# A two-layer graph network: a third set of buffers for the gathered rows of the edge network, with gathers issued three groups ahead

## What is computed

```python
h = concat([n_embed[senders], n_embed[receivers]], axis=-1)   # senders = src, receivers = dst
h = tanh(h @ W0 + b0)            # 512 -> 406
h = tanh(h @ W1 + b1)            # 406 -> 323
h = h @ W2 + b2                  # 323 -> 256
h = h * (e_embed @ Wg)           # e_embed: 50000 x 128
return segment_mean(h, senders, 50000)
...
x = layernorm(x + edge_network(x), axis=-1)
```

## Time and profile before

| | us |
|---|---|
| median of three timed executions | 4805.3 |
| lowest, highest of them | 4802.85, 4808.88 |
| profiled execution, first to last instruction (its span; no other time of it is given) | 4813.1 |
| busy: TensorE / VectorE / ScalarE / GpSimd | 3972.5 / 3729.6 / 3089.0 / 2981.9 |
| first gather of the edge network starts | 2698.73 |
| last scatter-add starts | 4504.97 |

### The profile page before, as it was taken

The page is one execution under the profiler, slowest core; times in us unless marked ns, Lnnn a source line. Parts: engine busy times, 40 slices in busy tenths (PEclk is TensorE's granted clock), DMA queues, the critical chain, the costliest instruction groups (busy, mean ns, idle before and its releaser), DMA issues. The chain is left out here.

```text
span 4813.1 us, 84225 instructions
## 1 busy us (share of the span) xinstructions
PE 3972.5 (83%) x23546; PEld 3291.7 (68%) x23546; DVE 3729.6 (77%) x11631; ACT 3089.0 (64%) x7157; POOL 2981.9 (62%) x2765
## 2 busy tenths in 40 slices
PE   5899999977777499999999799999999999999200
PEld 3466666655555399999999687777788778777200
DVE  6899999978888699898989476666666666666564
ACT  6866666645555266666666477776777767776575
POOL 1055556567777355555555377777777778777322
PEclk9999999988999699999999899999999999999655
DMA  4255554558666499999999577766767766766696
GB/s 105 51 171 169 168 171 167 169 148 212 199 201 202 151 360 364 349 365 353 365 359 362 175 152 154 153 149 153 152 150 153 154 152 149 153 150 152 218 394 261
DMA packets 717533, 1002.80 MB, mean 208 GB/s; under 512 B 186862, under 2 KB 591298, under 8 KB 704182
## 3 DMA queue, kind: packets, MB, share of 16 engines
q0 software_dynamic: 160768, 323.45, 30.3%
q10 hardware_dynamic: 245565, 375.01, 21.6%
q1 hardware_dynamic: 310861, 300.30, 19.8%
HBM read 567.01 MB, written 431.82 MB: 208 GB/s over the span
## 5 line engine op out<-in xcount | busy, mean ns | idle before, releaser
L1468 PE MATMUL bank<-w0r,n_x1T 128*128 128x406 f32 x4704 | 903.3, 351 | 41.1 <-ACT n_pa L1516 38.9
L1468 PEld LDWEIGHTS bank<-w0r,n_x1T 128*128 128x128 f32 x4704 | 868.0, 189 | 65.6 <-ACT n_pa L1516 63.4
L1612 POOL DMA_INDIRECT out_x<-u_sums,u_row x392 | 635.8, 1622 | 144.4 <-issue 117.1
L1664 PE MATMUL bank<-u_h,w1r 128*108 128x512 f32 (+1 forms) x2646 | 692.4, 407 | 0.0
L635 POOL DMA_INDIRECT DS<-payload,rank_int x392 | 378.2, 965 | 477.0 <-DVE rank_int L810 386.5
L1344 POOL DMA_INDIRECT n_cg<-CT,n_last x392 | 452.0, 1153 | 174.4 <-issue 95.2
L1664 PEld LDWEIGHTS bank<-u_h,w1r 128*108 128x108 f32 (+1 forms) x2646 | 444.5, 175 | 129.8
L1595 POOL DMA_INDIRECT u_pa<-PA,key_int x392 | 388.2, 990 | 167.2 <-issue 120.1
L891 POOL DMA_INDIRECT xg<-XP,ds x392 | 412.4, 1052 | 125.9 <-issue 121.3
L1664 PE MATMUL bank<-w2r,u_h 108*128 108x256 f32 x3528 | 479.2, 280 | 0.0
L427 PE MATMUL bank<-wst,xT 128*128 128x264 f32 x1568 | 421.3, 391 | 51.0 <-DVE xps L436 50.8
(11 more groups left out here) (319 smaller groups left out, 10080.4 us busy)
## 6 DMA issues: line engine op xcount, KB each, us to landing
PA<-n_pa ACTq DMA_DIRECT2D x98, 816.0 KB
PB<-n_pb ACTq DMA_DIRECT2D x98, 812.0 KB
XP<-xps ACTq DMA_DIRECT2D x98, 528.0 KB
CT<-ct ACTq DMA_DIRECT2D x98, 528.0 KB
n_xp<-XP SPq DMA_DIRECT2D x98, 528.0 KB
xin<-in_x SPq DMA_DIRECT2D x97, 512.0 KB
n_x<-in_x SPq DMA_DIRECT2D x97, 512.0 KB, 9.8
out_x<-n_x ACTq DMA_DIRECT2D x97, 512.0 KB, 5.0
```

Of the source, the lines that this page charges most:

```text
L1468: o = nc.tensor.matmul(acc, xT[s][p][:, k, e], w0r[q][:, 2 * half + k, :], start=(n == 0), stop=(n == len(terms) - 1))
L1612: pool.indirect_dma_start(out=out, out_offset=bass.IndirectOffsetOnAxis(ap=si[s][:, j:j + 1], axis=0), in_=yo[s][:, j, :], in_offset=None, ...
L1664: o = nc.tensor.matmul(acc, a[p], b[q], start=(start and n == 0), stop=(stop and n == 2))
```

## The change

Both buffer lists for gathered rows get three entries instead of two, group g uses set g % 3, and the semaphores `gath` become three. GpSimd issues the gathers of groups 0, 1 and 2 ahead of its first body, and in body g those of group g+3. `free(g)` waits for the sums and transposes of group g-3 instead of group g-2. VectorE clears the three right-hand ends of `u_pb` instead of two, and adds each group where it did. The other buffers, the pairs of scatter-adds and the order on TensorE, ScalarE and SyncE stay.

```diff
@@ -1547,8 +1547,9 @@
 
         ph = ExitStack()
         with ph:
-            pa = [alloc(ph, f"u_pa{s}", [P, G, AW]) for s in range(2)]
-            pb = [alloc(ph, f"u_pb{s}", [P, G, SW]) for s in range(2)]
+            SETS = 3
+            pa = [alloc(ph, f"u_pa{r}", [P, G, AW]) for r in range(SETS)]
+            pb = [alloc(ph, f"u_pb{r}", [P, G, SW]) for r in range(SETS)]
             rc = [alloc(ph, f"u_rc{s}", [P, G, 1]) for s in range(2)]
             ed = [alloc(ph, f"u_edge{s}", [P, G, P]) for s in range(2)]
             h1 = [[alloc(ph, f"u_h1{s}{q}", [P, 3, G * P], f32r) for q in range(2)] for s in range(2)]
@@ -1564,7 +1565,7 @@
             kb = [alloc(ph, f"u_keys{s}", [P, G * P], i32) for s in range(2)]
             si = [alloc(ph, f"u_row{s}", [P, G], i32) for s in range(2)]
             yo = [alloc(ph, f"u_sums{s}", [P, G, D]) for s in range(2)]
-            ed_ld, gath, o_st = sems("u_e_loaded"), sems("u_gathered"), sem("u_out_added")
+            ed_ld, gath, o_st = sems("u_e_loaded"), sems("u_gathered", SETS), sem("u_out_added")
             v_init, v_sum, v_chain, k_ld = sem("u_init"), sem("u_sum"), sem("u_chain"), sems("u_keys_loaded")
             p_t, p_e, p_l, p_q, p_c = (sem("u_transposed"), sem("u_e_transposed"), 
                                             sem("u_layer1"), sem("u_layer2"), sem("u_combined"))
@@ -1590,16 +1591,17 @@
 
                 @block.gpsimd
                 def _(pool):
-                    def gather(g, s, j):
+                    def gather(g, j):
+                        r = g % SETS
                         for q, (buf, table, w) in enumerate(((pa, PA, AW), (pb, PB, F0))):
                             pool.indirect_dma_start(
-                                out=buf[s][:, j, 0:w], out_offset=None, in_=table,
+                                out=buf[r][:, j, 0:w], out_offset=None, in_=table,
                                 in_offset=bass.IndirectOffsetOnAxis(ap=KI[:, 1 - q, g * G + j:g * G + j + 1], axis=0))\
-                                .then_inc(gath[s], 16)
+                                .then_inc(gath[r], 16)
 
                     def free(g):
-                        need(pool, v_sum, 4 * (g - 1))
-                        need(pool, p_t, 4 * (g - 1))
+                        need(pool, v_sum, 4 * (g - SETS + 1))
+                        need(pool, p_t, 4 * (g - SETS + 1))
                         pool.sem_inc(turn, 1)
 
                     def scatter(g, s, j):
@@ -1614,18 +1616,18 @@
                             in_=yo[s][:, j, :], in_offset=None, bounds_check=N - 1, oob_is_err=False,
                             compute_op=ALU.add).then_inc(o_st, 16)
 
-                    for g in range(2):
+                    for g in range(SETS):
                         free(g)
                         for j in range(G):
-                            gather(g, g, j)
+                            gather(g, j)
 
                     def body(g, s, i, last):
-                        if not late(g, 2):
-                            free(g + 2)
+                        if not late(g, SETS):
+                            free(g + SETS)
                         for h in range(G // 2):
                             for j in (2 * h, 2 * h + 1):
-                                if not late(g, 2):
-                                    gather(g + 2, s, j)
+                                if not late(g, SETS):
+                                    gather(g + SETS, j)
                             for j in (2 * h, 2 * h + 1):
                                 if not early(g, 2):
                                     scatter(g - 2, s, j)
@@ -1649,7 +1651,7 @@
                         n = NK[k]
                         a = k * P if k < 3 else TC
                         for j in range(G):
-                            o = nc.tensor.transpose(TB[k % 2][0:n, j * P:(j + 1) * P], pb[s][:, j, a:a + n], ident[:])
+                            o = nc.tensor.transpose(TB[k % 2][0:n, j * P:(j + 1) * P], pb[g % SETS][:, j, a:a + n], ident[:])
                         o.then_inc(p_t, 1)
 
                     def edges(g, s, i, last):
@@ -1812,8 +1814,8 @@
                 def _(dve):
                     c = Count(dve, v_chain)
 
-                    for s in range(2):
-                        c.did(nc.vector.memset(pb[s][:, :, F0:SW], 0.0))
+                    for r in range(SETS):
+                        c.did(nc.vector.memset(pb[r][:, :, F0:SW], 0.0))
                     c.did(nc.vector.memset(prior[:, 0:P], 1.0))
                     c.did(nc.vector.tensor_copy(prior[:, P:2 * P], upto[:]))
                     c.did(nc.vector.memset(h2[0][:, 2, :].bitcast(f32), 1.0))
@@ -1821,23 +1823,24 @@
                     c.wait()
                     base0 = c.n
 
-                    def add(g, s, k):
-                        a = slice(k * P, (k + 1) * P)
-                        nc.vector.tensor_tensor(pb[s][:, :, a], pb[s][:, :, a], pa[s][:, :, a], ALU.add).then_inc(v_sum, 1)
-
-                    def add_first(g, s, i):
-                        dve.wait_ge(gath[s], 32 * G * (i + 1))
-                        add(g, s, 0)
+                    def add(g, k):
+                        a, r = slice(k * P, (k + 1) * P), g % SETS
+                        nc.vector.tensor_tensor(pb[r][:, :, a], pb[r][:, :, a], pa[r][:, :, a], ALU.add).then_inc(v_sum, 1)
+
+                    def add_first(g):
+                        dve.wait_ge(gath[g % SETS], 32 * G * (g // SETS + 1))
+                        add(g, 0)
 
                     def add_rest(g, s):
-                        add(g, s, 1)
-                        add(g, s, 2)
+                        r = g % SETS
+                        add(g, 1)
+                        add(g, 2)
                         need(dve, a_g, 4 * (g - 1))
-                        nc.vector.tensor_copy(rc[s][:], pa[s][:, :, F0:F0 + 1])
+                        nc.vector.tensor_copy(rc[s][:], pa[r][:, :, F0:F0 + 1])
                         nc.vector.tensor_tensor(
-                            pb[s][:, :, TC:SW].rearrange("p t (k w) -> p t k w", k=3)[:, :, :, 0:R0],
-                            pb[s][:, :, A0:F0].unsqueeze(2).to_broadcast([P, G, 3, R0]),
-                            pa[s][:, :, A0:F0].unsqueeze(2).to_broadcast([P, G, 3, R0]), ALU.add).then_inc(v_sum, 1)
+                            pb[r][:, :, TC:SW].rearrange("p t (k w) -> p t k w", k=3)[:, :, :, 0:R0],
+                            pb[r][:, :, A0:F0].unsqueeze(2).to_broadcast([P, G, 3, R0]),
+                            pa[r][:, :, A0:F0].unsqueeze(2).to_broadcast([P, G, 3, R0]), ALU.add).then_inc(v_sum, 1)
 
                     def low0(g, s, k):
                         dve.wait_ge(a_hk, 4 * g + k + 1)
@@ -1916,16 +1919,16 @@
                         message(g, s, 2)
                         low_message(g, s, 1)
                         if not late(g, 2):
-                            add_first(g + 2, s, i + 1)
+                            add_first(g + 2)
                         message(g, s, 3)
                         low_message(g, s, 2)
                         low_message(g, s, 3)
                         if not late(g, 2):
                             add_rest(g + 2, s)
                     dve.wait_ge(v_init, 1)
-                    add_first(0, 0, 0)
+                    add_first(0)
                     add_rest(0, 0)
-                    add_first(1, 1, 0)
+                    add_first(1)
                     add_rest(1, 1)
                     for k in range(4):
                         low0(0, 0, k)
```

## The result

The kernel with three sets took **4829.34 us** (median of 5 runs, 4825.32 to 4833.7), the kernel before 4805.3 us (5 runs): ratio 1.0042, 95% interval 1.0027 to 1.0057. It is slower by 20 us by the ratio, by 24 by the medians. Its profiled execution spans 4829.8 us. The forecast was 4798.4 us, with a range of 4782 to 4821; rival A had been priced at 4829 us.

The account below looks back on a forecast made before the run. GpSimd's full instruction stream was taken to bound the edge network. The end 6.9 us earlier and net 0 from collisions, off the 4805.3 us median, gave 4798.4 us, range 4782 to 4821.

Parts of the forecast that it names:

- rival A: GpSimd's starts at L1595 and L1612 under L1826: new phase hits, 0.52 us a body, +24, 4829 us; chance 0.20.
- What bounds: Edge network: GpSimd's instruction stream is full, 18.0 us a group; its 20% idle is issue time, TensorE would go faster.
- Start: First bodies: 24 gathers fill the first idle piece, 3.30 and 6.28 us remain; one group of gathers more behind GpSimd.
- Steady part: Full bodies of eight gathers and four scatter-adds: 93 instead of 94, still 18.04 us each.
- End: Bare scatter-add pairs after the last body: ten instead of eight, 6.61 us each; the stage ends 6.9 us earlier.
- The wait that takes its place: VectorE slides 1.65 us or a little more earlier, then stops at scatter_rows' wait for scatter-adds to land; pace stays GpSimd's.
- The size of GpSimd's own instructions: Collisions with VectorE's two-SBUF-input operations stay at 0.19 us a body, net 0; bounds -17.4 to +31 us.

Follow-up runs that it names:

- e4: Kernel before, with the second table's gathers left out for each group's last tile (zeros instead): 4693.63 us, ratio 0.976.
- e3: Changed kernel, with SyncE's two 256 KB loads held until the scatter-adds of the group three before theirs have landed: 4816.98 us, ratio 1.0019.
- e8: Changed kernel with three sets of u_row and u_sums, VectorE's first addition also awaiting GpSimd's increment before a body's first gather: 4814.55 us, ratio 1.0014 to kernel before.
- e9: As e8, with the increment two gathers later in GpSimd's queue: 4845.54 us, ratio 1.008 to the kernel before.
- e5: Kernel before, with a 128 x 784 memset on VectorE between the wait for gathers and a group's first addition: 4871.34 us, ratio 1.0132.

## Why the prediction was wrong

*What bounds.* Right: e4 shows it directly, and no piece of GpSimd's idle time in the middle is over 1.2 us (six wait for `u_sums`, 4.6 us in all).

*Start.* Right in kind. The 24 gathers filled the first piece and most of the second (1.08 us left, 3.3 forecast); body 2 began 57.5 us after the first gather, before 57.3.

*Steady part.* The count was right (93 bodies), the pace not.

*End.* Ten bare pairs came, at 6.75 us each instead of 6.61 (three of their ten waits, the first among them, are 3.6 to 3.8 us long instead of 3.2), which gives 1.9 us less gain than the sum had.

*The wait that takes its place.* The place was right, "and then stops at this wait" was not. It rested on landings of at most 4.5 us, read from one pair at the end; the kernel before has up to 4.95 in the middle. The slide that it allowed also brought VectorE's selection forward, which releases SyncE's two loads, and these came to lie right behind the scatter-adds and delayed their landing to about 6 us. I had priced the landing as given and not asked what VectorE's earlier work sets off. The runs without SyncE's early loads (e3) hold VectorE still.

*The size of GpSimd's own instructions.* **This is the step that failed.** "I take the old 0.19 us ... Net 0" measured (1702.6 - 93 x 17.86) / 93 = 0.45 us a body, +24.9 us over the forecast 93 bodies; of these some 21.6 us are in the three means (4 x (41 + 13 + 4) ns x 93), the rest in short idle pieces. -6.9 + 24.9 + 1.9 = +19.9 us, and the stage is 20.1 us longer. The argument for it was that the old and the new burst both have three or four starts in them, mostly between instructions; the starts struck went from 69 to 166 in 1400 us. The old phase was no average one. Being released by the landing of a gather, whose time is fixed against GpSimd's stream, puts the first addition within 0.2 us of the start of a scatter-add in 64 of 78 bodies; every other phase tried here costs more. That "each hit pushes GpSimd later and off the edge" stood on no row.

*Rival A* had the mechanism, hits in the new phase, but expected one bad phase in every body. The runs with a fixed phase cost less (e3, e8) or more (e9) than the changed kernel, whose phase wanders. That its price, 4829 us, is the measured time is in part luck: it stood on 0.52 us a body and on no loss at the end. Its threshold, 0.36 us a body, was passed with 0.45.

The Trainium skill, SBUF — State Buffer, section Who interferes with whom, holds that a two-input tensor_tensor was not seen to stall a GpSimd DMA. The rows of e8 and e9 contradict it in size and in time: the lengthening is the rest of the operation, less 0.12 us. By that rule e8 and e9 would take the same time; they differ by 31 us.

## What to carry to other kernels

Before adding a buffer, look at whether the engine that issues the transfers has any gap to use; where its stream is full, a wait elsewhere is only the slack of the others. Such a wait may also be holding two engines in a phase that suits them: when a change removes it, price the phases it frees and not only the old one, and follow what the released engine sets off (here the loads of SyncE). Two kernels that differ only in the place of one semaphore increment test phase alone; here that decided, and a memset as a delay did not.

## What the runs showed of the hardware

- A GpSimd indirect DMA whose start falls 0.05 us or more into a VectorE operation with two SBUF inputs takes longer by what is left of that operation less 0.12 us (0.24, 0.19, 0.51 and 0.52 us in the four cases shown). Over the 166 struck DMAs counted above in the changed kernel the rest less the lengthening is 0.08 to 0.13 us in the middle 80%. An operation that begins 0.02 us behind the DMA's start costs nothing (e8). A memset of 784 columns cost 1.25 us together with the addition behind it, though by its row it began 0.13 us behind the start (e5).
- Two loads of 256 KB from SyncE, the first issued 0.04 to 0.65 us and the second 0.45 to 1.06 us behind a scatter-add's start, moved its landing from 3.9 to 5.9 us in the median (24 groups of 65 above 5 us). With the first 1.2 us behind or later (e8) the median is 4.5 us and none is above 5; with the loads held back until the scatter-add had landed (e3) it is 3.8.
- GpSimd's queue runs ahead of its DMAs: an increment that stands in front of a body's first gather released VectorE 3.74 us before the preceding scatter-add even started (e8).
